# Causal operands stored for six transfers a half, bf16 class values, loops written out, and a new order of TensorE's work in the quantized feed-forward

## The reference, cut to what matters

```
# block 0
x   = norm(norm(tok(x)) @ (sf_w*mask).T ...) + ...          # pass_tokens
q,k,v = norm(x) @ wq.T, wk.T, wv.T                          # pass_qkv, 16 heads of 16
att = relu(q k^T / 4) * causal ; att /= sum(att) + 1e-9     # pass_causal
x   = x + (att v) @ wo.T ; x = x + relu(norm(x) @ f1) @ f2  # pass_mlp
xq  = fp4_quant_dequant(z)                                  # pass_fp4, blocks of 16
h   = silu(xq @ wg.T) * (xq @ wu.T) ; out = fp4_quant_dequant(h) @ wd.T
# block 1: a state-space layer (pass_ssm_in, pass_scan), then a gate over
# experts (pass_moe) and softmax attention (pass_attend), over 513 tokens
```

## Time and profile before

| | |
|---|---|
| median of 3 runs | 2281.74 us (2280.27 to 2282.27) |
| the profiled execution's own time | 2278.18 us, its span 2276.4 us |
| PE, DVE, ACT, POOL busy | 92%, 70%, 40%, 32% of the span |
| mean granted clock of TensorE | 0.955 |
| DMA | 132.43 MB, 58 GB/s over the span |
| pass_qkv, PE's first to last matmul | 184.6 to 306.7 us |
| pass_causal, first scores to last turn | 328.0 to 552.0 us |
| pass_mlp, pass_fp4 | 554 to 865 us, 866 to 1188 us |
| pass_moe, pass_attend | 1384 to 1796 us, 1799 to the end |

### The profile page before, as it was taken

One profiled execution on the slowest core, in us unless ns is written; L12 is line 12 of the kernel. 1 busy time (PEld: TensorE's weight loads), 2 busy tenths in 40 slices (PEclk: granted clock), 3 DMA queues, 4 the chain that ended last, 5 costly groups with the idle time before them and its releaser, 6 DMA issues. The chain is left out here.

```text
span 2276.4 us, 41030 instructions
## 1 busy us (share of the span) xinstructions
PE 2098.8 (92%) x11587; PEld 1337.9 (59%) x11587; DVE 1594.1 (70%) x4366; ACT 907.1 (40%) x2124; POOL 737.6 (32%) x1350
## 2 busy tenths in 40 slices
PE   7998969998999997999988958999999999999998
PEld 6886833333888885666663316888888523333332
DVE  3336846665677776888866856776777788888882
ACT  1114635553221223444433431222222157777777
POOL 3554525554333332333422101111111423333222
PEclk9998979998999999999998968999999779999999
DMA  4323665443000000000001010212214302232210
GB/s 135 114 90 86 152 181 144 138 133 108 1 0 0 0 0 14 1 0 0 0 24 37 9 31 20 48 37 47 46 38 125 89 10 76 81 95 78 76 44 20
DMA packets 215394, 132.43 MB, mean 58 GB/s; under 512 B 116675, under 2 KB 204309, under 8 KB 215317
## 3 DMA queue, kind: packets, MB, share of 16 engines
q1 hardware_dynamic: 215316, 131.50, 21.4%
HBM read 89.81 MB, written 41.25 MB: 58 GB/s over the span
## 5 line engine op out<-in xcount | busy, mean ns | idle before, releaser
L2547 DVE TENSOR_REDUCE attend_mx<-ps 128x1 f32<-128x512 f32 x512 | 320.9, 682 | 40.5 <-PE ps L2241 39.4
L2384 ACT ACTIVATE attend_w<-ps 128x512 f32<-128x512 f32 x512 | 280.6, 596 | 92.5 <-PE ps L2255 90.7
L1854 PE MATMUL ps<-keep_early,moe_zT 128*128 128x256 f32 x1056 | 243.4, 384 | 6.4 <-DVE keep_h L2009 4.4
L1854 PEld LDWEIGHTS ps<-keep_early,moe_zT 128*128 128x128 f32 x1056 | 196.5, 191 | 43.1 <-DVE keep_h L2009 18.6
L2241 PE MATMUL ps<-keep_x,keep_o 96*128 96x512 bf16 x512 | 209.8, 416 | 5.7 <-DVE attend_mx L2547 4.0
L2255 PE MATMUL ps<-keep_o,keep_x 99*128 99x512 bf16 x512 | 191.6, 384 | 2.7 <-ACT attend_w L2384 2.7
L2009 DVE SCALAR_TENSOR_TENSOR keep_h<-ps,moe_g,keep_h 128x256 f32 (+1 forms) x264 | 127.6, 483 | 61.5 <-PE ps L1854 53.2
L863 DVE SCALAR_TENSOR_TENSOR keep_early<-ps,causal_causal 128x512 f32<-128x512 f32 (+3 forms) x256 | 114.0, 486 | 80.2 <-PE ps L743 80.1
L2241 PEld LDWEIGHTS ps<-keep_x,keep_o 96*128 96x128 bf16 x512 | 50.3, 99 | 183.8 <-DVE attend_mx L2547 136.0
L833 POOL TENSOR_TENSOR keep_early<-keep_early,causal_causal 128x128 f32<-128x128 f32 x256 | 113.3, 458 | 128.7 <-ACT keep_early L802 127.7
L802 ACT ACTIVATE keep_early<-ps 128x512 f32<-128x512 f32 (+3 forms) x256 | 98.5, 435 | 126.3 <-PE ps L743 126.0
(11 more groups left out here) (332 smaller groups left out, 4064.2 us busy)
## 6 DMA issues: line engine op xcount, KB each, us to landing
tok_xin<-in_xk SPq DMA_DIRECT2D x64, 256.0 KB, 2.7
qk_parts<-qkv_parts SPq DMA_DIRECT2D x33, 384.0 KB, 3.2
qk_parts<-moe_parts SPq DMA_DIRECT2D x33, 384.0 KB, 3.2
causal_qs<-qk_parts SPq DMA_DIRECT2D x96, 128.0 KB, 2.7
causal_ks<-qk_parts SPq DMA_DIRECT2D x96, 128.0 KB, 2.7
keep_o<-qk_parts SPq DMA_DIRECT2D x96, 128.0 KB, 2.8
keep_x<-qk_parts SPq DMA_DIRECT2D x96, 128.0 KB, 2.8
v_all<-qkv_v SPq DMA_DIRECT2D x33, 136.0 KB, 3.1
```

What stands on the lines that cost most here:

```text
L1854: last = nc.tensor.matmul(ps[:, E0 + pair % 2, e % 2 * D:(e % 2 + 1) * D], zT[:, u, k * P:(k + 1) * P], we[e][:, k, :], start=(k == 0), st ...
L2384: nc.scalar.activation(w[:, j, kt % 2, :], ps[:, SC + (HG * k + j) % RING, :], ACT.Exp)\
L2547: nc.vector.tensor_reduce(mx[:, t, k:k + 1], ps[:, MX + (TB * k + t) % RING, :], AX, ALU.max)\
```

## The change

- `tiles()` in pass_qkv, pass_mlp, pass_fp4, pass_moe and for POOL in pass_ssm_in writes out all 33 tiles; pass_causal writes out its eight images. pass_tokens keeps its hardware loops (`looped_tiles`).
- q and k rows are stored (element, head) within a half, in six slots: q parts in slots 0, 1, 2 and k parts in 5, 4, 3. Three runs of slots give the six pairs, so `load_stacks` issues 3 transfers for q and 3 for k, of 48, 32 and 16 partitions. The splitting instructions write through `part_of`, a view by blocks of 128. Both pass_causal and pass_attend load this way.
- Class weights are split into three bf16 parts: ACT writes one more tile (fp32 and bf16), POOL runs `class_parts`, three instructions of [16, 128] with waits between, once a tile, and once `class_value`, four of [1, 272]. The class value matmul is then one bf16 product of K = 96 against a block-diagonal `vb`.
- The first half's stacks, its values, the constants of pass_causal (the mask and 12 pieces of `vb`) and the first class weights are loaded by SP during pass_qkv, at tiles 27, 28 and 29. What pass_causal did at its start for `vbd` (four loads, a PE and a DVE step) goes.
- Stacks of a later image are loaded when the scores of that half are done, no longer when its values are done.
- In pass_fp4 PE's order is turn_z(s), gate_up(s, 0), turn_h(s-3), gate_up(s, 1), down(s-3).

```diff
+RUNS = ((0, 3), (3, 2), (5, 1))
+def part_of(parts, u, c):
+    return parts[:, u, :, c:SLOTS - c:SLOTS - 1 - 2 * c, :].rearrange("p m q t -> p q m t")
+def load_stacks(sp, io, m, b, qs, ks, sem):
+    for at, n in RUNS:
+        rows = slice(0, 2 * HD * n, 2) if at == 0 else slice(2 * HD * (at - 3) + 1, 2 * HD * (at - 3 + n), 2)
+        for dst, slot in ((qs, 0), (ks, SLOTS - n)):
+            src = io["qk_parts"][m, slot:slot + n, :, bass.ds(1 + TB * b, TB), :].rearrange("c (d h) n t -> (c d) h (n t)", d=HD)
+            sp.dma_start(dst[rows, :, :], src).then_inc(sem, 16)
...
 # pass_qkv, SP
+                if isinstance(s, int) and s == NT - LATE:
+                    ahead.first.load_stacks(sp, io, 0)
+                if isinstance(s, int) and s == NT - LATE + 1:
+                    ahead.first.load_values(sp, io, 0)
+                    ahead.load_constants(sp, io)
+                if s == NT - LATE + 2:
+                    ahead.load_class(sp, io, 0)
...
 # pass_qkv, POOL
+            def class_parts(s):
+                pool.wait_ge(s_cls, s)
+                ch.link(nc.gpsimd.tensor_tensor(cls_r[:, :], cls_s[:, u, :], cls_p[:, u, 0, :], ALU.subtract))
+                ch.link(nc.gpsimd.tensor_copy(cls_p[:, u, 1, :], cls_r[:, :]))
+                nc.gpsimd.tensor_tensor(cls_p[:, u, 2, :], cls_r[:, :], cls_p[:, u, 1, :], ALU.subtract).then_inc(s_clsp, 1)
+                pool.wait_ge(s_clsp, s)
...
                 if known(s) >= 3:
                     third(s - 3, 1 - u)
+                if known(s) == 3:
+                    class_value()
+                if known(s) >= 5:
+                    class_parts(s - 4)
...
 # pass_causal
-                nc.tensor.matmul(ps[:, 4 + g % 2, :], vbd[:, HG * g:HG * (g + 1), :].rearrange("h a d -> h (a d)"),
-                                 cls_w[:, g // 2, :], start=True, stop=False, skip_group_check=True)
+                nc.tensor.matmul(ps[:, 4 + g % 2, :], vb[:, g // 2, at:at + 2 * HD * HG], ahead.cls[:, b % 2, :],
+                                 start=True, stop=False, skip_group_check=True)
...
 # pass_fp4, PE
-            for s, u, n in tiles(pe, 5):
+            for s, u, n in tiles():
                 turn_z(s)
+                gate_up(s, 0)
                 if known(s) >= 3:
                     turn_h(s - 3)
-                gate_up(s, 0)
+                gate_up(s, 1)
                 if known(s) >= 3:
                     down(s - 3)
-                gate_up(s, 1)
```

More of the change, by code:

```diff
@@ L654, in _ @@
                 value(s, s % 2, s // 2)
[L658 to L674, removed]
@@ new lines, with __init__, reserve, load_constants @@
+class Causal:
+    def __init__(self, nc):
+        self.area = Area(nc, "first")
+        self.s_stacks, self.s_values, self.s_cls = (self.area.sems(n, 2) for n in ("stacks", "values", "cls"))
+        self.s_const = self.area.sem("const")
+    def reserve(self):
+        self.first = Half(self.area, 0, self.s_stacks[0], self.s_values[0])
+        self.causal = self.area.sb("causal", [P, S])
+        self.vb = self.area.sb("vb", [NH * SLOTS, 2, HALF * 2 * HD], BF16)
+        self.cls = self.area.sb("cls", [NH * SLOTS, 2, S], BF16)
+    def load_constants(self, sp, io):
+        sp.dma_start(self.causal[:, :], io["causal"]).then_inc(self.s_const, 16)
+        for at, n in RUNS:
+            for c in range(n):
+                for half in range(2):
+                    row = NH * (at + c) + HALF * half
+                    sp.dma_start(self.vb[row:row + HALF, half, :],
+                                 io["diag_parts"][n - 1 - c, 0, half, 0:HALF * HALF * 2 * HD].rearrange("(h x) -> h x", h=HALF))\
+                        .then_inc(self.s_const, 16)
+    def load_class(self, sp, io, b):
+        for at, n in RUNS:
+            sp.dma_start(self.cls[NH * at:NH * (at + n), b % 2, :],
+                         io["cls_parts"][0:n, :, TB * b:TB * (b + 1), :].rearrange("c h n t -> (c h) (n t)"))\
+                .then_inc(self.s_cls[b % 2], 16)
@@ L683, in pass_causal @@
     ps = env.ps
-    R = HD * len(PQ)
+    R = HD * SLOTS
     with a.ctx:
[L686 to L694, removed]
+        ahead = env.causal
+        halves = [ahead.first, Half(a, 1, ahead.s_stacks[1], ahead.s_values[1])]
+        s_stacks, s_values, s_const, causal, vb = ahead.s_stacks, ahead.s_values, ahead.s_const, ahead.causal, ahead.vb
+        v0 = a.sb("v0", [B, NH * (HD + 1)])
         prod = a.sb("prod", [P, KD, B])
@@ L789, in _ @@
             batch(0, first=True)
-            with pe.Fori(1, B) as b:
+            for b in range(1, B):
                 batch(b)
@@ L820, in _ @@
             batch(0, first=True)
-            with act.Fori(1, B) as b:
+            for b in range(1, B):
                 batch(b)
@@ L826, in _ @@
         def _(pool):
-            with pool.Fori(0, B) as b:
+            pool.wait_ge(s_const, CONSTS)
+            for b in range(0, B):
                 for g in range(NG):
@@ L1621, in _ @@
         def _(pool):
-            for s, u, n in tiles(pool):
+            for s, u, n in tiles():
                 ln.on_pool(pool, s, u)
@@ L2613, in build @@
         for step in PASSES:
-            step(nc, env, io)
+            if step is pass_qkv:
+                env.causal = Causal(nc)
+                with env.causal.area.ctx:
+                    env.causal.reserve()
+                    pass_qkv(nc, env, io)
+                    pass_causal(nc, env, io)
+            elif step is not pass_causal:
+                step(nc, env, io)
 PASSES = [pass_constants, pass_tokens, pass_qkv, pass_causal, pass_mlp, pass_fp4, pass_ssm_in, pass_scan, pass_moe,
```

262 lines of the change are left out of this document (168 added, 94 removed).

## The result

The changed kernel takes 2302.64 us (median of four, 2301.51 to 2303.9) against 2281.28 for the kernel before, run on the same chip: a ratio of 1.0094, 95% interval 1.0076 to 1.0111, 21 us slower.

| from, to | before | after | |
|---|---|---|---|
| pass_qkv, first to last transpose | 184.6 to 298.5 | 185.6 to 318.4 | +18.9 |
| last root of pass_qkv to SP's next stage | 295.6 to 314.6 | 316.4 to 346.4 | +11.0 |
| SP's first issue to the scores | 314.57 to 328.00 | 346.42 to 347.16 | -12.7 |
| pass_causal, first scores to last turn | 328.0 to 551.7 | 347.2 to 540.8 | -30.1 |
| pass_fp4, first to last add of h | 907.7 to 1188.3 | 896.6 to 1216.1 | +38.9 |

What follows compares the result with a forecast made beforehand. PE was taken to bound the kernel, 92% busy. Front +7 (+12 +1 +6 -12), class value -28, pass_fp4 +40, loops -3 sum to +16 us: 2298 us, range 2266 to 2325, chance of the forecast 0.60.

Steps and rivals of the forecast that it cites:

- POOL in pass_qkv: In pass_qkv: class_parts makes POOL the bound at 4.0 us a tile, above PE's 3.56; +12 us, bounds 6 and 24.
- the fourth rival: In pass_qkv: DVE's two-input instructions hold POOL, period 4.7 instead of 4.0 us; +20, 2318 us; chance 0.08.
- `class_value`: In pass_qkv: four chained POOL instructions of 272 columns, 2.9 us, once, add 1 us.
- The tail: End of pass_qkv: SP's 23 more issues at tiles 27 to 29 make stores late; +6 us, 0 to 9.
- The start of pass_causal: Start of pass_causal: with stacks, values and constants in place, scores follow the small product; 12 us saved.
- Class value: In pass_causal: 32 class value matmuls on PE each save 0.85 us; with fewer issues -28 us, bounds -18 and -30.
- pass_fp4: PE's new order: up waits for DVE's product, circle down, add_h, product, up; period 10.4 instead of 9.03 us; +40, bounds 25 and 46.
- the one behind it: In pass_fp4: circle through ACT, silus behind take_hT, then snap, POOL's scaling, turn_z, zT; 9.7 to 9.9 us around.
- Loops written out: All written-out stages: 64 loop iterations go, each end costing nothing to 0.18 us; -3 us.
- the harmless order: In pass_fp4: the new order is harmless or better, PE alone sets 8.9 us; -3 us in the stage, 2255; chance 0.12.
- the full front: Front of pass_causal wins all its 12 us, POOL's new instructions being cheaper or overlapped; sum -2, 2280 us; chance 0.13.
- TensorE's granted clock: Rival in pass_fp4: PE only 81% busy, so its clock falls to 0.87; +22, 2320 us; chance 0.07.

## Why the prediction held, and where its sizes were off

Forecast were +16 us and 2298; it is 21 us and 2302.6. That the sum came so near is in part luck: up to the scores of pass_causal the forecast had +7 and the trace has +19; from there on it had +9 and the trace has +5, since the loops and the class value gave more than forecast and pass_fp4 cost a little less. One error covers a part of the other. By its steps:

- **POOL in pass_qkv.** POOL becomes the bound as forecast, and PE waits for the apply behind the root. The forecast of the period was 4.0 us; it is 4.22 or 3.89. The sum behind the 4.0 was wrong in two terms that cancel in part. The copy was put at 0.28 us, right for an idle DVE, and takes 0.84 beside DVE's subtraction of two fp32 inputs, or takes 0.28 and gets the last subtraction 0.65 instead of 0.42. And POOL's old instructions with their starts were put at 2.26 us, and take 1.9 (0.19, 0.55 and 1.15). Without the hold the tile would be 4.22 - 0.56 = 3.66 us, an estimate that the tile without L728 bears out, only 0.1 above PE's 3.56. So the fourth rival's mechanism is there and makes most of the price, at 0.56 or 0.23 us a tile instead of the 0.7 on top of 4.0. The waits (0.17, 0.18, 0.24) and the subtractions (0.47, 0.42 against 0.41) were as reckoned; POOL is busy for 83%, not over 90%, since its waits for itself do not count. The Trainium skill, GPSIMD Engine Reference, section 8, Key points, names DVE instructions with two SBUF inputs as a source of contention; these rows agree.
- **`class_value`.** Put at +1 us; the root behind it comes 2.7 us later than before (9.80 instead of 7.12 us behind the one ahead). Its four instructions take 0.41, 1.24, 0.40 and 0.69 us, the 1.24 where 0.69 was reckoned. The stage as a whole is +14.9 to +18.9 instead of +13.
- **The tail.** +11.0 instead of +6, and outside the bounds of 0 to 9. I counted SP's issues and took the late stores from them; what holds the stores is the data ahead of them, 1.5 MB at a full DMA (share 1.08, 244 GB/s), and then the fallen clock. The spread prefetch, with the same issues, took 7.7 of the 11 us away.
- **The start of pass_causal.** -12.7 against -12: scores 0.74 us after SP's first issue.
- **Class value.** -30 against -28, and the group of 5.91 us was forecast as 5.9. But 32 groups by 0.82 us are only 26. Of the rest, 1.8 us are in the first group (9.77 us before, 7.17 after), which both kernels begin at a granted clock of 0.50, and some 2 us in groups of the kernel before that took 6.8 to 7.5 us. No run undoes the class value alone.
- **pass_fp4.** Period 10.39 against 10.4, and 40 us by the run that undoes the order. The circle is the one drawn, and so is the one behind it: 9.7 with the add moved. Idle PE ahead of up (1.2 us, 33 in the stage) and of gate (0.46) is where it was said to be; snap still waits for ACT (0.84); only ACT's wait was no part of the price.
- **Loops written out.** -3 was too small: pass_mlp and pass_moe are 3 us shorter each, the run with loops again is 8 us slower with the old order, and in the new order the loops would cost another 8 in pass_fp4, since there the loop's end lies in the circle. This pays for a part of what the front of the kernel lost over the forecast.
- **The rest.** From the end of pass_fp4 to the first scores of pass_attend 5 us are gained and in pass_attend 2 are lost; 3 of the 5 are the shorter pass_moe.

Of the rivals, the harmless order falls with the run that undoes it, and the full front with the 18.9 and 11.0 us. TensorE's granted clock is 1.00 in pass_fp4, where PE was busy for 84% of the time; it fell in the tail of pass_qkv, where PE did nothing for 3 us.

## What to carry to other kernels

An order of one engine's work is judged by the circles that it closes: follow the last waiting instruction through each queue that stands behind something else, add up the way round, and do the same again for the circle behind the longest, for it decides what a repair is worth. Moving work to an idle engine puts it behind that engine's own waits; place it ahead of them, or the move can close a new circle. Where two instructions that hold each other start at nearly the same time, one trace does not give the period: look at several. Large prefetches go in one at a time among the stores that somebody waits for, not in one piece before the end of a stage.

## What the runs showed of the hardware that was not expected

- A small POOL copy tripled beside a DVE subtraction of two fp32 inputs (0.28 to 0.84 us), and a POOL subtraction went from 0.42 to 0.63; beside DVE's L755, which reads one input from PSUM, that one took 0.42 (253.23 in the run with the copy on ACT). With starts 0.02 to 0.03 us apart it was now POOL's copy that got longer and now DVE's subtraction (0.67 to 0.80), the former 7 to 19 times among 32 tiles; with 7 the transposes of the stage spanned 128.8 us, with 19 they spanned 132.8.
- The issue of the values' store holds SP for some 0.75 us in a steady tile, for up to 1.5 us behind one stack transfer of the spread prefetch, and for 4.23 us behind six. The Trainium skill, DMA: Bandwidth & Descriptors, section Queues, rings and completion order, says that a sequencer's copies share one row of rings, each consumed in order; the store that landed late behind the stacks agrees.
- Written-out code adds transfers that the profile calls "instruction": between 220 and 296 us the changed kernel has 4 on queue 8 and 7 on queue 14, the kernel before none. ACT's waits for stores at 261.0 and 298.0 us stand within 4 us behind a fetch of queue 8, while two other fetches of that queue (236 and 278 us) cost no wait; such waits went when the loops of PE and DVE came back. These are single traces, and no run changes the fetches alone, so that they cause the waits is likely, not shown. The price is small here, 3 to 4 us in the stage, and the loops' ends cost as much.

```profile
q8 instruction: 4, 0.07, 0.3%
q14 instruction: 7, 0.06, 0.2%
```
